# Four edits to a graph network kernel: 16-bit tables, beta moved, an index kept, another attention order

## The reference

```python
# layer 0: messages of edges with features
e   = mish(x[src] + edges @ W_e_k + W_e_b)
agg = segment_sum(e, dst)
h   = relu(concat((1 + eps) * x + agg, g) @ W1 + b1) @ W2 + b2
# layer 1: two mean aggregations          layer 2: normalised sums, batch norm over the nodes
h   = relu(h @ W_self + mean(h[src]) @ W_neigh + b);  h / norm(h)
# layer 3: attention with H = 8 heads of 16
q, k, v = x @ Wq + bq, x @ Wk + bk, x @ Wv + bv;  e = edge_attr * We
alpha = sum(q[dst] * (k[src] + e), per head) / 4
ex    = exp(alpha - segment_max(alpha, dst)[dst])
agg   = segment_sum(ex / denom[dst] * (v[src] + e), dst)
out   = layernorm((agg + skip) @ Wo + bo + x) * gamma + beta
```

## Time and profile before

| | us |
|---|---|
| median of 3 runs | 2227.64 (2219.5 to 2228.99) |
| profiled execution | 2228.31 |
| its span | 2226.6 |
| mean granted TensorE clock | 0.785 of full speed |
| busy: TensorE | 1354.5 (61%) |
| busy: VectorE | 1067.3 (48%) |
| busy: GpSimd | 1046.1 (47%) |
| busy: ScalarE | 943.8 (42%) |
| gathers of keys and values (L1766), 392 | 388.0 busy, 262.0 idle before them |
| scans of the maxima (L1867), 56 | 22.9 busy, 218.0 idle before them |

### The profile page before, as it was taken

The page is one execution under the profiler, slowest core; times in us unless marked ns, Lnnn a source line. Parts: engine busy times, 40 slices in busy tenths (PEclk is TensorE's granted clock), DMA queues, the critical chain, the costliest instruction groups (busy, mean ns, idle before and its releaser), DMA issues. The chain is left out here.

```text
span 2226.6 us, 31431 instructions
## 1 busy us (share of the span) xinstructions
PE 1354.5 (61%) x7918; PEld 1101.4 (49%) x7918; DVE 1067.3 (48%) x2945; ACT 943.8 (42%) x2003; POOL 1046.1 (47%) x1184
## 2 busy tenths in 40 slices
PE   4412236766667789699989996314454454444567
PEld 2200014434455568599989994214344443434555
DVE  4411149874344467555964215214344444434666
ACT  0100137774444568275526645313333333334324
POOL 5577710004666640024558342674655566565233
PEclk9555559888888899999989997657667677667886
DMA  4222212224555563074545451555666666665521
GB/s 148 62 68 52 67 59 89 104 95 152 164 174 178 185 208 101 13 257 158 187 159 206 146 184 52 149 143 160 190 191 173 187 193 188 188 175 174 168 62 37
DMA packets 214478, 314.19 MB, mean 141 GB/s; under 512 B 31638, under 2 KB 160149, under 8 KB 214224
## 3 DMA queue, kind: packets, MB, share of 16 engines
q1 hardware_dynamic: 111130, 153.97, 21.8%
q0 software_dynamic: 33488, 81.02, 13.0%
q10 hardware_dynamic: 69734, 77.65, 10.9%
HBM read 223.87 MB, written 88.67 MB: 140 GB/s over the span
## 5 line engine op out<-in xcount | busy, mean ns | idle before, releaser
L372 POOL DMA_INDIRECT fr_ring<-table,src_i x392 | 374.9, 956 | 412.7 <-SPq L649 277.4
L1766 POOL DMA_INDIRECT e_kv<-kv_table,e_idx x392 | 388.0, 990 | 262.0 <-DVE e_msg L1852 146.4
L679 PE MATMUL fe_ps<-fe_space 128*128 128x400 bf16 x591 | 175.9, 424 | 243.9 <-issue 153.4
L679 PEld LDWEIGHTS fe_ps<-fe_space 128*128 128x128 bf16 x591 | 86.1, 146 | 333.1 <-issue 307.5
L770 DVE TENSOR_SCALAR fe_space<-fe_space,fr_key 128x400 bf16<-128x400 f16 x591 | 159.0, 325 | 173.6 <-remote 64.8
L1801 PE MATMUL e_p<-e_msg,e_mask 128*128 128x144 f32 x784 | 141.4, 346 | 146.8 <-issue 103.8
L998 POOL CAST ly_af<-ly_au 128x640 fp32r<-128x640 uint16 x240 | 163.2, 726 | 127.4 <-DVE ly_part L1403 61.1
L1801 PEld LDWEIGHTS e_p<-e_msg,e_mask 128*128 128x128 f32 x784 | 130.7, 240 | 159.8 <-issue 139.5
L1780 PE MATMUL e_q<-e_qs,e_mask 128*128 128x136 f32 x784 | 148.2, 360 | 87.4 <-issue 62.4
L725 ACT ACTIVATE fe_space<-fe_ps 128x800 uint16<-128x800 f32 x100 | 83.5, 835 | 257.9 <-PE fe_ps L679 167.4
L1832 ACT ACTIVATE e_row<-e_p 128x864 f32<-128x864 f32 x56 | 49.5, 884 | 334.4 <-remote 292.3
(11 more groups left out here) (396 smaller groups left out, 3068.4 us busy)
## 6 DMA issues: line engine op xcount, KB each, us to landing
ly_au<-edge_counts SPq DMA_DIRECT2D x88, 800.0 KB, 4.6
sums_att<-e_row ACTq DMA_DIRECT2D x56, 532.0 KB
q_starts<-fe_space SPq DMA_DIRECT2D x56, 476.0 KB
e_qs<-q_starts SPq DMA_DIRECT2D x56, 476.0 KB
fe_edge<-in_edgesT ACTq DMA_DIRECT2D x98, 256.0 KB
edge_counts<-fe_space ACTq DMA_DIRECT2D x25, 800.0 KB
e_drow<-dst_short SPq DMA_DIRECT2D x56, 224.0 KB
fr_ring<-table,src_i POOLq DMA_INDIRECT x392
```

The costliest lines, as they stand in the source:

```text
L372: pool.indirect_dma_start(f.ring[:, n % RB, t, 0:D], None, tab[0][:, :], bass.IndirectOffsetOnAxis(ap=src_i[:, at:at + 1].bitcast(U32), ax ...
L679: nc.tensor.matmul(ps[:, bass.ds(at, NW)], left(n), right(n % IS), start=False, stop=True, skip_group_check=True).then_inc(c["item"], 1)
L1766: pool.indirect_dma_start(kv[s][:, t, :], None, kv_table[:, :], bass.IndirectOffsetOnAxis(ap=idx[s][:, t:t + 1].bitcast(U32), axis=0)).the ...
```

## The change

Four edits:

1. `front_tables`: the tables, the one-hots and the begun flags are 16-bit floats (all values are whole numbers below 2048 there), ScalarE makes a 16-bit copy of the ones matrix first, and the widths go from 591 to 592.
2. `middle`: the thirteen additions of beta leave GpSimd's list; VectorE makes five, of five node tiles each, after its last piece of the stage. SyncE's wait for them at the end goes.
3. `firstu` is worked out in `prepare` by VectorE from a tensor that is loaded there; the load, the limit and GpSimd's wait at the start of attention go.
4. `edges_attention`: the lags and the order of the sections change on TensorE, ScalarE and VectorE.

```diff
+firstu = sb("firstu", [TP, TK], U32)
...
+  dve.tensor_scalar(firstu[:, :], ht[:, :, 4], float(NP - 1), None, ALU.min)
...
- part = spare[0:shape[0], used[0]:used[0] + size]
- used[0] += -(-size // 8) * 8
+ words = -(-size // 2) if dt == F16 else size
+ part = spare[0:shape[0], used[0]:used[0] + words]
+ used[0] += -(-words // 8) * 8
- part = part if dt == F32 else part.bitcast(dt)
+ part = part if dt == F32 else part.bitcast(dt)[:, 0:size]
...
-tables = tmp("tables", [NF, 3, TF, P])
+tables, ones_h = tmp("tables", [NF, 3, TF, P], F16), tmp("ones_h", [P, P], F16)
+halved = sem("ft_halved")
-begun, node_begun = tmp("begun", [HB, 2, ITEMS]), tmp("node_begun", [NT, FI])
+begun, node_begun = tmp("begun", [HB, 2, ITEMS + 1], F16), tmp("node_begun", [NT, FI])
-blocks, at_tile, elsewhere = tmp("blocks", [P, ITEMS]), tmp("at_tile", [NF, ITEMS]), tmp("elsewhere", [P, ITEMS])
-chosen, number = tmp("chosen", [NF, TF, ITEMS]), tmp("number", [NF, TF])
+blocks, at_tile, elsewhere = tmp("blocks", [P, ITEMS + 1]), tmp("at_tile", [NF, ITEMS + 1]), tmp("elsewhere", [P, ITEMS])
+chosen, number = tmp("chosen", [NF, TF, ITEMS + 1], F16), tmp("number", [NF, TF])
-count, part = tmp("count", [P, ITEMS]), tmp("part", [P, 1])
+count, part = tmp("count", [P, ITEMS + 1]), tmp("part", [P, 1])
-split = [slice(0, BANK), slice(BANK, ITEMS)]
+split = [slice(0, BANK), slice(BANK, ITEMS + 1)]
...
-  pool.iota(count[:, :], [[1, ITEMS]], base=0, channel_multiplier=0,
+  pool.iota(count[:, :], [[1, ITEMS + 1]], base=0, channel_multiplier=0,
...
+  nc.scalar.activation(ones_h[:, :], ones[:, :], ACT.Copy).then_inc(halved, 1)
...
-  after(dve.tensor_copy(blocks[:, :], ps_a[:, 0:ITEMS]))
+  after(dve.tensor_copy(blocks[:, :], ps_a[:, 0:ITEMS + 1]))
...
-  after(dve.tensor_copy(turn[:, 0:ITEMS], blocks[0:1, :]))
+  after(dve.tensor_copy(turn[:, 0:ITEMS], blocks[0:1, 0:ITEMS]))
...
-  after(dve.tensor_tensor(elsewhere[:, :], ps_a[:, 0:ITEMS], blocks[:, :], ALU.not_equal))
+  after(dve.tensor_tensor(elsewhere[:, :], ps_a[:, 0:ITEMS], blocks[:, 0:ITEMS], ALU.not_equal))
...
+  pe.wait_ge(halved, 1)
-    summed = nc.tensor.matmul(ps_a[:, part_i], ones[0:HB, :], begun[:, c, part_i], start=(c == 0), stop=(c == 1))
+    summed = nc.tensor.matmul(ps_a[:, part_i], ones_h[0:HB, :], begun[:, c, part_i], start=(c == 0), stop=(c == 1))
...
-c = Counts(sem, "md", "relu back sq root floor inv res stat var std rstd shift norm tr at mm q kv skip beta")
+c = Counts(sem, "md", "relu back sq root floor inv res stat var std rstd shift norm tr at mm q kv skip")
...
-  sp.wait_ge(c["beta"], NG)
...
-   if n % 2 == 0:
-    c.ready(pool, "tr", n // 2)
-    here = x_now[:, n:min(n + 2, NT), :]
-    pool.tensor_tensor(here, here, bc[:, B_B3:B_B3 + 1, :].broadcast_to([P, min(2, NT - n), D]), ALU.add).then_inc(c["beta"], 1)
...
+  c.ready(dve, "tr", NG - 1)
+  for a in range(0, NT, NS):
+   dve.tensor_tensor(x_now[:, a:a + NS, :], x_now[:, a:a + NS, :], bc[:, B_B3:B_B3 + 1, :].broadcast_to([P, NS, D]), ALU.add)
...
-first_in, first_u, first_out = sem("e4_first_in"), sem("e4_first_u"), sem("e4_first_out")
-firsts, firstu = (st.enter_context(nc.sbuf_tensor(f"e4_{k}", [TP, TK], dt)) for k, dt in (("first", I32), ("firstu", U32)))
+first_out = sem("e4_first_out")
...
-  with nc.allow_non_contiguous_dma(reason="five numbers per edge tile"):
-   sp.dma_start(firsts[:, :], headtail[:, :, 4]).then_inc(first_in, 16)
...
-  pool.wait_ge(first_u, 1)
...
-  pipelined(pe, NB, KS, [(4, total), (2, back), (0, fill), (1, turn)])
+  pipelined(pe, NB, KS, [(2, turn), (2, back), (3, total), (1, fill)])
...
-  pipelined(act, NB, KS, [(0, masks), (4, exp), (5, evac), (5, store)], head=2)
+  pipelined(act, NB, KS, [(0, masks), (2, exp), (3, evac), (3, store)], head=2)
-  dve.wait_ge(first_in, 16)
-  dve.tensor_scalar(firstu[:, :], firsts[:, :], float(NP - 1), None, ALU.min).then_inc(first_u, 1)
...
-  pipelined(dve, NB, KS, [(4, message), (3, differ), (2, maxima), (0, breaks), (1, scores)], head=2)
+  pipelined(dve, NB, KS, [(2, scores), (3, message), (2, maxima), (1, breaks), (2, differ)], head=2)
```

## The result

The changed kernel took 2257.84 us (median of 4, 2246.12 to 2264.72) against 2227.69 (median of 4, 2219.5 to 2228.99): a ratio of 1.0129, 95% interval 1.0084 to 1.0173. It is slower by 30 us, where I had forecast 113. The sign held, the size didn't.

A forecast was written before the change was run, and what follows sets the result against it. Attention was taken as bound by TensorE's signals reaching VectorE late while GpSimd gathers. Attention +130, edits 1 to 3 -11.5, -1.5 and -4.0: +113 on 2228.3, so 2341 us, range 2170 to 2440.

The forecast's parts named there:

- The closed loop: New attention order: scores, message, scans, back, total and fill in series; 8.9 us at full clock, 10.6 with gathers, 9.5 without.
- the first rival: Attention: signals pass in the new order, turn 10.0 us, 93 us faster, 2135 us; chance 0.25.
- the walk of one turn: Attention with gathers: the transpose's signal passes, fill ends at 10.6 us, fq arrives at the run's end, about 14; 14.3 taken.
- the second estimate of 16.3: Attention with gathers: the loop's growth added to today's turn, 12.0 + (10.6 - 6.3) = 16.3 us.
- The last turns: Attention behind the last gather: 8 turns of 9.5 us, 76 us for 45, +31.
- The first message: Start of attention: shorter lags bring the first message forward by a step of about 8 us.
- Edit 1: Tables stage: 16-bit products end it at 61 us in place of 72.5, gain 11.5, bounds 9.5 and 12.3.
- It would end at 57.2: Tables stage: VectorE's list of small steps, ending at 59.73, ends 2.5 us sooner after a shorter first sum.
- Everything behind waits at the stage's end, so it is carried through: Tables stage: its whole gain of 11.5 us reaches the kernel's total time.
- Edit 2: Middle stage: VectorE's five adds take 3.7 us, GpSimd's scatters end sooner; gain 1.5 us, bounds 0 and 3.
- comes out even: Rival in attention: turn 11.7 to 12.1 us, no change in time; chance 0.05.
- the forecast's 12.8 to 16: Attention's turn with gathers in the forecast's own case, 2270 to 2420 us; chance 0.58.

The follow-up runs named there:

- the stretches of 14: No separate run: three times in the changed kernel's slower trace GpSimd made 14 gathers; mid-stretch fq was 0.04, 0.04 and 0.22 us late, the next 4.4, 4.4 and 5.5.
- the run of 56: No separate run: 56 gathers at attention's start in the changed kernel's slower trace; scores began 10.6 us after fill's end with 44 us of gathers to come.
- prompt chips: The four chips of the experiments: kernel before 1722 to 1725 us; with the new order, scores begin 0.04 us after fill's end at the median.
- first conditions: Those of the first pair of kernels, met by no experiment again, chip not recorded: kernel before 2227.69 us, changed kernel 2257.84.
- fill first: Changed kernel with TensorE's list as fill, turn, back, total, same lags: 1710.37, 1708.33 and 1712.85 us, ratios 0.9917, 0.9910 and 0.9930 against the kernel before.

## Why the prediction was right in sign and wrong in size

**The closed loop** is right, piece by piece. Forecast for 0.70 clock: message done at 3.7, back at 4.65 to 5.1, fill's end at 10.6, GpSimd on its way at 4.5. In the turn shown, counted from 1803.19: 3.71, 4.64 to 4.96, 11.02, and 4.50. For turns without gathers I had 9.5 us; from 2128.77 the next scores come at 2139.19 and 2149.30, 10.3 a turn, at a granted clock of 0.74 and not the 0.88 of the earlier trace rows. Taking total out of the loop and taking the gathers away (7.54 and 10.13) show, for prompt signals, that the loop, and not the gathers, sets the new turn: it is the loop's 10.1 us. That is the first rival's turn of 10.0, and yet the kernel is slower there, because the old order then runs at 8.93 and not at 12.0.

**The step that failed** is in the walk of one turn: "signals no longer pass, and fq arrives when the run ends, about 14", from which I took 14.3 us and 47 x (14.3 - 12.0) = +107. Measured, 48 turns of 12.39 against 11.95, +21. The loop's part of the turn was right, fill's end at 10.57 us on average where I had 10.6. The mis-sized term is fq's lateness, for which 14.3 leaves 3.7 us: it was 1.84 on average and 1.5 at the median (0.04 to 4.4 us, 5.5 and 9.3 in one turn each). In 37 of the 48 turns scores began before the run of gathers was over, in 17 of them 1.3 to 1.4 us before its end, some 0.4 us before its last gather began; in the other 11 they began behind it. I had put the run's end at 13.5 (it is 13.05), rounded the walk up, and then gone up again toward the second estimate of 16.3, which added the loop's growth to a turn that was already long for another reason. A delay up to about the run's end is short when runs are seven gathers and fill ends late in them. So the mechanism, a TensorE signal delayed while GpSimd gathers, was there; its size was 1.8 us a turn, half of what I had. That a signal always waits for the run's end, as the walk had it, is not so (the stretches of 14 and the run of 56 above).

**The other half of that step** is what the 14.3 is compared with. The old order's turn held lateness itself: over the whole stage 11.03 us against 8.93 on the prompt chips, 2.1 us. The new order lost 1.9 (10.09 to 12.01), most of it lateness and some 0.4 a longer way through total and fill (fill's end at 10.57 us after the scores against 10.16). Both orders pay about the same for the first conditions, so the difference between them is near that of the loops against the gathers. I had named the one that pays more as the new one.

**The last turns**: +33, forecast +31. **The first message**: 13.6 us sooner in the stage, forecast 8 for the order and 4 for edit 3.

**Edit 1**: -6.8 where I had 11.5, bounds 9.5 to 12.3. The last table's 512-column products are single records and it takes 2.15 us (2.4 forecast), 5.3 less than before. "It would end at 57.2" is the step that failed: from L524 to L536 VectorE's small steps leave it idle for up to 1.9 us between two of them, and the list ends at 60.5, later than the 59.73 of before, although its input came sooner. That the path before was VectorE's list and not TensorE's tables was misread as well: the last table waited for the second table's records, which ended at 63.64, when VectorE had been done with its input at 61.42. Now VectorE is the last, and the last table begins 1.2 us sooner (62.22 for 63.43). These rows are of the kernel before:

```profile
59.29 4.34 PE L582 MATMUL ft_b<-fr_ring 98*128 98x512 f32 x11 [0.39 <-issue]
...
60.65 0.77 DVE L539 CAST fr_lo<-ft_a 128x591 f16<-128x591 f32 x1
```

And these of the changed one:

```profile
54.90 0.27 DVE L532 TENSOR_TENSOR fr_ring<-fr_ring 1x122 f32<-1x122 f32 x1 [0.48 <-DVE fr_ring L531]
56.31 0.21 DVE L533 TENSOR_SCALAR fr_ring<-fr_ring 1x122 int32<-1x122 int32 x1 [1.14 <-DVE fr_ring L532]
...
58.40 0.21 DVE L534 TENSOR_SCALAR fr_ring<-fr_ring 1x122 int32<-1x122 f32 x1 [1.88 <-remote]
59.10 0.27 DVE L535 TENSOR_TENSOR fr_take_words<-fr_ring 1x122 int32<-1x122 int32 x1 [0.49 <-DVE fr_ring L534]
59.81 0.21 DVE L536 TENSOR_SCALAR fr_ring<-fr_ring 1x122 int32<-1x122 f32 x1 [0.44 <-DVE fr_take_words L535]
...
62.22 2.15 PE L588 MATMUL ft_a<-fr_ring 98*128 98x512 f16 x8 [14.79 <-DVE fr_lo L544]
```

"Everything behind waits at the stage's end, so it is carried through" failed too. The lead was still 6.6 us at the first message of layer 0 and gone at the last (L824 against L818: 497.2 against 503.8, then 901.9 against 902.1). The granted clock in windows placed alike was 0.76 against 0.84 at the widest (644 to 694, before 650 to 700) and 0.94 against 1.00 (794 to 844, before 800 to 850). Whether that is chance or answers to the lead is open: each side has one profile. On the prompt chips this stage, which no edit touches, took 545.0 to 549.9 us in 13 profiles, so 6 us is little more than its scatter there; the tail, -3.5 us here, took 92.4 to 97.9.

**Edit 2**: -5.0, bounds 0 to 3. The adds cost 3.75, as worked out (3.7). The stage ends 0.9 us behind them, so of the 3.0 us between the last scatter's row and the next stage up to 2.1 was landing, where I had taken 1.5. The larger part is a term that I had at nothing: VectorE's last piece ended 2.2 us sooner (1410.86 for 1413.05) in a stage that began 0.5 later. 2.1 and 2.7 make 4.8 of the 5.0. By the same 2.1 us the last scatter landed as the adds ended, near 1414.5, so which of the two ended the stage can't be told.

**Edit 3**: 3.5 us (4.3 to 0.8 after the stage's start), forecast 4.0.

**The chances.** The case that came, a turn of 12.4 in this stretch, lies between "comes out even" (11.7 to 12.1) and the forecast's 12.8 to 16, in a gap that no case held; the range of 2170 to 2440 did hold 2257.84. The Trainium skill's "DMA: Bandwidth & Descriptors", section "Anatomy of one DMA", gives about 100 ns for the semaphore update at the end of a DMA; it says nothing of TensorE's signals. Taken for them all the same, as in the prediction, it would make the turn the loop's: that is near the prompt chips (0.04 us at fq, 10.1 us a turn) and not the first conditions (1.8 us).

**What stays open**: what made signals late in the first conditions, and whether fill first helps there. One thing beside the chip differs: for the same changed kernel the trace of the first conditions holds 14361 records of semaphore updates and 8675 of DMA landings, the one of a prompt chip 29866 and 23173. Whether what lost the records also held up the engines, and whether an execution without the profiler would be late at all, no run tests. Edits 1 to 3 with fill first are 0.7 to 0.9% faster than the kernel before on two prompt chips, and so are edits 1 to 3 with the old lists (0.7 to 0.8%); between these two nothing can be told, since both wait for GpSimd.

## What to carry to other kernels

Before a pipeline's lags are shortened, write down for each engine which sections of one step stand in its queue ahead of the one that the next step needs: here two sections that fill did not need, back and total, stood ahead of it in the queue, and one place in a list was worth 2.6 us a turn (without gathers, on a prompt chip). A shorter distance in steps bought some 10 us once, at the stage's start (13.6 with edit 3), and was paid for in 55 turns. And a delay in the profile that is as large as a quarter of the time should be measured on a second chip before anything is built around it.

## What the runs showed of the hardware

- The same kernel took 2228 us in the first conditions and 1722 to 1725 on four chips. The difference is in the stages where GpSimd gathers in long runs: the kernel before took 870.5 us for layer 0 and 708.8 for attention, while on prompt chips the first took 545 to 550 and the second, with the old order and edits 1 to 3, 540 to 542. Layers 1 and 2, without gathers, took 402 and 400 to 405. Yet the gathers keep their pace: 40 of them stand in the same 50 us of either (200 to 250). Beside them the front stage made 18 one-hots and on a prompt chip 141 (changed kernel there, L776, 200 to 250 us):

```profile
200.00:250.00 50.00, 38.53 (x141) 0.86 0.44 148
```

- In the first conditions VectorE started on a grid of 0.70 us while GpSimd gathered. The one-hots of L770 in the kernel before that had idle time ahead of them stand 2.1, 2.8, 3.5 us and so on apart: 72 of 72 distances below 7 us, between 75 and 480 us, are multiples of 0.70 to within 0.06.

```profile
212.33 0.32 DVE L770 TENSOR_SCALAR fe_space<-fe_space,fr_key 128x400 bf16<-128x400 f16 x1 [2.48 <-remote]
215.12 0.33 DVE L770 TENSOR_SCALAR fe_space<-fe_space,fr_key 128x400 bf16<-128x400 f16 x1 [2.47 <-remote]
217.93 0.32 DVE L770 TENSOR_SCALAR fe_space<-fe_space,fr_key 128x400 bf16<-128x400 f16 x1 [2.48 <-issue]
220.03 0.32 DVE L770 TENSOR_SCALAR fe_space<-fe_space,fr_key 128x400 bf16<-128x400 f16 x1 [1.78 <-PE fe_ps L679]
```

- Late signals were not only TensorE's: VectorE's own, from one small step to its next, came 0.4 to 1.9 us late (rows of L532 to L536 above, again 0.7, 1.4 and 2.1 us from start to start), the last of them over 3 us behind the last gather's row, which ends at 56.4. On a prompt chip the same steps leave no idle time of 0.1 us between them, beside the same gathers. And TensorE stood for 2.2 us twice inside the second table's products of the kernel before (at 55.09 and 57.89), where its list has no wait.
- Where TensorE stood more it was granted less clock. Without gathers the new order's turns were granted 0.78, with TensorE busy for 57% of the time, and the old order's 0.92, with 71%; the old one does nearly the same products in 340 us that take 557 in the new (windows of either, whole run of messages):

```profile
1120.00:1677.00 557.00, 316.77 (x1625) 292.83 (x1625) 282.19 (x762) 240.63 (x588) 44.48 (x48) 0.78 0.67 204
```

```profile
1140.00:1480.00 340.00, 242.47 (x1600) 214.78 (x1601) 272.27 (x752) 223.39 (x573) 44.48 (x48) 0.92 0.99 325
```

Total takes 1.98 us in the earlier trace rows and 3.49 in the prompt turn above, in the loop. That the loop's gaps lower the clock and so lengthen the loop fits these rows; no run varies the gaps alone.
